# A conditioning stage on one core: caps moved from VectorE to ScalarE, forward scans made in place

## The chip, the cores and the metric

One Trainium2 chip, one of its cores. The metric is the device time of one execution in microseconds (us); lower is better. Engines: PE is TensorE, DVE VectorE, ACT ScalarE, POOL GpSimd, SP the queue that issues most transfers.

## What is computed

Four batches of 512 tokens with 512 channels pass through one layer: a bidirectional recurrence over the tokens ("conditioning"), a gated recurrence with four 512x512 projections, a second conditioning of the result, and a mixture of 8 experts with 2 chosen per token. Both conditionings share their input k = v = `fside`, and differ in the per-channel vectors w and u. The change lies in them:

```
tf    = sigmoid(sum(cond))                       # one number per batch
decay = exp(-exp(w)) * (0.5 + 0.5 * tf)          # per channel and batch
ek    = exp(minimum(k, 30.0));  ekv = ek * v
df, nf = forward scans  a = a * decay + ek (ekv)
db, nb = the same scans from the last token to the first
euk   = exp(minimum(u + k, 30.0))
num   = nf + nb - ekv + euk * v
den   = df + db - ek + euk
out   = sigmoid(r) * num / maximum(den, 1e-8) * (0.8 + 0.2 * tf)
```

All of it is float32.

## The kernel before, in words

The program has two phases. The first makes the two conditionings, the gated recurrence, the logits and the places of the tokens, and sends the rows to the experts' slots in HBM; the second computes the experts. The change is in the first alone.

**Units.** Channels lie on the 128 partitions, tokens along the free dimension, so a batch is four tiles of 128x512, called units here (u = 4b + ct, 16 in all). Since k doesn't depend on the layer, a unit makes both conditionings c = 0 and 1 together: four sums (numerator n = 0 and denominator n = 1 of each c) in `sums_even` or `sums_odd`, by the parity of the unit. Every other buffer of a unit is double too, except `recip0` and `scaled`.

**A unit, engine by engine.** PE transposes f into `ps_f`; ACT copies it to `kT` (`copy_f`, L539). DVE makes the caps (`caps`): min(k, 30) into `ek` (L745) and min(k + u, 30) into `euk` for each c (L747). ACT takes exp of both in place (`exps`, L552, L553). POOL multiplies by k: `ekv` (L332), `eukv` for each c (L334, L335). DVE scans backward over the tokens (`backward`, L784 for ek, L785 for ekv, for each c). The recurrence forward then runs over the backward sums: with b the backward sum, the two-sided sum s obeys s[t] = d * s[t-1] + (1 - d*d) * b[t], with s[0] = b[0]. So ACT writes (1 - d*d) * b to `scaled` (`scale`, L562, one instruction of 128x1022 for each c), and DVE scans it forward into `sums` (`fold`, L796, four scans of 511 columns). The per-channel decay is read from PSUM (`ps_decay`). DVE adds `euk` to both denominators (L800, L801) and takes the maximum with 1e-8 for both in one instruction (L803), which signals `s_den`. ACT makes a first reciprocal as exp(-ln(den)) (`first_reciprocal`, L572, L575); POOL adds the own term to the numerators and multiplies twice by it (`newton`, L343, L346, L347, for each c); DVE forms the quotient (`ratio`, L812) after a Newton step.

**Order.** Each engine runs a list written out by hand; semaphores join them. In a step DVE does, for the units s = 0 to 3: `backward`, `caps` of the next unit, `fold`, then the ratios of unit s - 1. ACT does `copy_f` of the next unit, `first_reciprocal` of unit s - 1, `scale` of s, `exps` of the next. POOL does `newton` of unit s - 1, then `products` of unit s + 1. Behind these lines stand the rest of the step: step b also makes the gates of batch b - 1 (PE `gate`, L428; ACT L590, L601; DVE `recurrence`, L829 to L832) and the output rows and routing of batch b - 2 (DVE `residual` after the first backward, L839; `second_out` after fold 1, L844; `select` after fold 2, L853 to L868; `place` at the end; POOL `dispatch`, L365). At a step's end stand the last ratios and `first_out` (L821). Steps 0 to 3 have conditioning, steps 1 to 4 gates, steps 2 to 5 the tail. Steps 2 and 3 are one loop in the program.

The list on ACT around the change (`unit(s)` in `step`, L647 to L654) is:

```
copy_f(b if s + 1 < CT else b + 1, (s + 1) % CT)
if s >= 1: first_reciprocal(b, s - 1)
scale(b, s)
exps(b if s + 1 < CT else b + 1, (s + 1) % CT)
```

## Time and profile before

| | |
|---|---|
| time, median of 3 runs | 1264.4 us (1262.67 to 1265.08) |
| the profiled execution's own time, its span | 1265.84 us, 1263.7 us |
| busy: PE, weight loads, DVE, ACT, POOL | 1051.8, 830.8, 693.6, 527.8, 306.5 us |
| mean granted clock of TensorE, share of full speed | 0.939 |
| 14 to 88 us (step 0): DVE busy | 68.7 of 74.0 us |
| 260 to 350 us (step 3): DVE busy | 82.8 of 90.0 us |
| 350 to 420 us (steps 4 and 5 in part): PE, DVE busy | 68.7, 34.8 of 70.0 us |
| first expert matmul | 475 us |

Times in the profile are from the span's start. A busy share over the whole span mixes the two phases: PE is busy for most of the second, DVE for most of the first four steps. An instruction's time in the trace includes what it waited for inside the engine, so the same form can have two lengths.

### The profile page before, as it was taken

The numbers are of one execution on the slowest core, as the hardware profiler recorded it, in microseconds if no ns is written. First come the engines' busy times: TensorE is split into PE (matmuls) and PEld (weight loads), VectorE is DVE, ScalarE is ACT, GpSimd is POOL, SyncE is SP. The second block draws the span as 40 slices with busy tenths as digits, with TensorE's granted clock in tenths as the row PEclk, the third lists the DMA queues.
The fourth block names the chain that finished last, engine by engine and source line by source line (L and its number), as shares of the span: only waits on it lengthen the run. The fifth ranks groups of instructions, "written<-read, shape, count | busy, mean of one in ns | idle before, by whom it ended". The sixth has DMA issues, their size and how long they took to land.

```text
span 1263.7 us, 16714 instructions
## 1 busy us (share of the span) xinstructions
PE 1051.8 (83%) x5058; PEld 830.8 (66%) x5059; DVE 693.6 (55%) x1026; ACT 527.8 (42%) x845; POOL 306.5 (24%) x251
## 2 busy tenths in 40 slices
PE   1045886886899719999999999999897997999994
PEld 0022343433457519998999899889786886988883
DVE  6989899899872523334333433445454343333553
ACT  5354645835844202334233333334454333333453
POOL 4767727547530230001000200020202002000202
PEclk9998897987998759999999999999998998999997
DMA  7151150111021351114311622253535135211721
GB/s 245 39 160 34 65 182 32 67 68 66 0 82 43 145 202 68 66 67 127 89 66 66 151 101 97 103 115 133 157 130 171 66 133 140 69 66 66 189 87 20
DMA packets 63420, 125.53 MB, mean 99 GB/s; under 512 B 4726, under 2 KB 4762, under 8 KB 63384
## 3 DMA queue, kind: packets, MB, share of 16 engines
q1 hardware_dynamic: 54728, 107.91, 24.5%
q0 software_dynamic: 8656, 17.13, 6.7%
q8 instruction: 24, 0.39, 0.1%
q14 instruction: 12, 0.10, 0.0%
HBM read 93.04 MB, written 35.22 MB: 101 GB/s over the span
## 4 chain that ended last, share of the span: by engine, by line
PE 57%; issue 4%; ACT 1%; POOL 0%; DVE 0%; DVEq 0%; ACTq 0%; POOLq 0%
PE ps_h L1099 9%; PE ps_h L1101 9%; PE ps_y L1110 9%; PE ps_h L1100 9%; PE ps_y L1111 9%; PE ps_y L1112 9%; PE ps_t L1073 1%; POOL out_dram L1052 0%; ACT xh L1209 0%; ACT y L1216 0%; ACT w1h L1181 0%; DVE w1l L1232 0%; DVEq L1154 0%; DVE hl L1271 0%; DVEq L105 0%
## 5 line engine op out<-in xcount | busy, mean ns | idle before, releaser
L1099 PE MATMUL ps_h<-xh,w1h 128*128 128x320 f32 (+3 forms) x768 | 250.7, 326 | 38.2 <-issue 36.3
L1101 PE MATMUL ps_h<-xh,w1l 128*128 128x320 f32 (+3 forms) x768 | 246.3, 321 | 0.0
L1100 PE MATMUL ps_h<-xl,w1h 128*128 128x320 f32 (+3 forms) x768 | 246.2, 321 | 0.0
L1271 DVE SCALAR_TENSOR_TENSOR hl<-ps_h,hh 128x320 fp32r<-128x320 f32 (+1 forms) x192 | 107.0, 558 | 229.0 <-ACT hh L1205 224.3
L1052 POOL DMA_INDIRECT out_dram<-y,token x40 | 63.2, 1579 | 692.2 <-ACT y L1216 514.9
L1110 PE MATMUL ps_y<-w2h,hh 128*128 128x512 f32 (+1 forms) x528 | 206.8, 392 | 1.0 <-DVE hl L1271 1.0
L1111 PE MATMUL ps_y<-w2h,hl 128*128 128x512 f32 (+1 forms) x528 | 206.8, 392 | 0.0
L1112 PE MATMUL ps_y<-w2l,hh 128*128 128x512 f32 (+1 forms) x528 | 206.0, 390 | 0.0
L1205 ACT ACTIVATE hh<-ps_h 128x320 fp32r<-128x320 f32 (+1 forms) x192 | 94.3, 491 | 266.8 <-PE ps_h L1101 266.6
L1235 DVE TENSOR_TENSOR w2l<-raw,w2h 128x512 fp32r<-128x512 f32 x128 | 88.5, 692 | 198.0 <-ACT w2h L1184 197.1
L428 PE MATMUL ps_mm<-r1T,wm 128*128 (+1 forms) x320 | 162.3, 659 | 21.3 <-ACT z_in L590 14.4
L1099 PEld LDWEIGHTS ps_h<-xh,w1h 128*128 128x128 f32 x768 | 148.0, 193 | 47.2 <-issue 38.2
L1184 ACT ACTIVATE w2h<-raw 128x512 fp32r x128 | 80.8, 631 | 211.6 <-PE ps_y L1112 211.6
L1100 PEld LDWEIGHTS ps_h<-xl,w1h 128*128 128x128 f32 x768 | 148.0, 193 | 5.0
L1101 PEld LDWEIGHTS ps_h<-xh,w1l 128*128 128x128 f32 x768 | 147.6, 192 | 2.7
L428 PEld LDWEIGHTS ps_mm<-r1T,wm 128*128 128x128 f32 x320 | 66.0, 215 | 96.9 <-issue 79.5
L1112 PEld LDWEIGHTS ps_y<-w2l,hh 128*128 128x128 f32 (+1 forms) x528 | 96.6, 183 | 24.3
L1111 PEld LDWEIGHTS ps_y<-w2h,hl 128*128 128x128 f32 (+1 forms) x528 | 96.6, 183 | 19.7
L1110 PEld LDWEIGHTS ps_y<-w2h,hh 128*128 128x128 f32 (+1 forms) x528 | 96.6, 183 | 19.3 <-DVE hl L1271 1.3
L1232 DVE TENSOR_TENSOR w1l<-raw,w1h 128x512 fp32r<-128x512 f32 x128 | 88.4, 690 | 16.2 <-ACT w1h L1181 12.4
L1181 ACT ACTIVATE w1h<-raw 128x512 fp32r x128 | 79.8, 623 | 0.0
L365 POOL DMA_INDIRECT slots<-r_rows,dest x32 | 35.0, 1095 | 103.9 <-DVE dest L890 61.2
(190 smaller groups left out, 1291.4 us busy)
## 6 DMA issues: line engine op xcount, KB each, us to landing
raw<-in_L_ffn_w_dram SPq DMA_DIRECT2D x64, 1024.0 KB
slots<-r_rows SPq DMA_DIRECT2D x8, 1302.5 KB, 15.2
rows<-slots SPq DMA_DIRECT2D x8, 1302.5 KB, 9.1
f_rows<-in_fside_BxSxS_dram SPq DMA_DIRECT2D x5, 1024.0 KB, 5.4
rows<-in_x_dram SPq DMA_DIRECT2D x4, 1024.0 KB, 6.2
out_dram<-x_rows SPq DMA_DIRECT2D x4, 1024.0 KB, 5.3
slots<-r_rows POOLq DMA_DIRECT2D x1, 1302.5 KB
rows<-slots SPq DMA_DIRECT2D x5, 260.5 KB, 3.9
```

Source lines behind the costliest of these rows:

```text
L428: last = nc.tensor.matmul(ps_mm[:, k % 3, :], wm[:, m, dt, e * P:(e + 1) * P], r1T[:, bass.ds(b % 2, 1), dt, :].rearrange("p o t -> p (o t)"),
L1099: nc.tensor.matmul(o, w1h[:, j, dt, :], xh[:, dt, lo:hi], start=(dt == 0), stop=False)
L1100: nc.tensor.matmul(o, w1h[:, j, dt, :], xl[:, dt, lo:hi], start=False, stop=False)
L1101: last = nc.tensor.matmul(o, w1l[:, j, dt, :], xh[:, dt, lo:hi], start=False, stop=(dt == CT - 1))
L1110: nc.tensor.matmul(ps_y[0:m, i, :], hh[:, j, tok], w2h[:, j], start=first, stop=False)
L1111: nc.tensor.matmul(ps_y[0:m, i, :], hl[:, j, tok], w2h[:, j], start=False, stop=False)
L1112: done = nc.tensor.matmul(ps_y[0:m, i, :], hh[:, j, tok], w2l[:, j], start=False, stop=last)
L1184: a.activation(w2h[:, (j + 1) % 2], raw2[:, bass.ds((c + (j + 1) // FC) % 2, 1), (j + 1) % FC] .rearrange("p o n -> p (o n)"), ACT.Copy).t ...
L1205: a.activation(hh[:, j % 2, lo:hi], ps_h[:, bank, 0:hi - lo], ACT.Relu).then_inc(s_hh, 1 if wide else 2)
L1232: v.tensor_tensor(w1l[:, j % 2], raw1[:, bass.ds((c + j // 2) % 2, 1), :, (j + 2) % FC * P:((j + 2) % FC + 1) * P] .rearrange("p o t q -> ...
L1235: v.tensor_tensor(w2l[:, (j + 1) % 2], raw2[:, bass.ds((c + (j + 1) // FC) % 2, 1), (j + 1) % FC] .rearrange("p o n -> p (o n)"), w2h[:, ( ...
L1271: v.scalar_tensor_tensor(out=hl[:, j % 2, lo:hi], in0=ps_h[:, bank, 0:hi - lo], scalar=0.0, in1=hh[:, j % 2, lo:hi].bitcast(F32), op0=ALU.max,
```

## The change

The sums are carried divided by 1 - d*d. The forward scan then reads the backward sum itself, s[t] = d * s[t-1] + b[t], in place; only column 0 of the four sums is multiplied by 1 / (1 - d*d) first (new L802). `scale` and its buffer go. The own term gets the same divisor inside its exp: `euk` is exp(30 - ln(1 - d*d) - relu(30 - u - k)), and the floor 1e-8 becomes a number per channel (`den_min`), so the maximum is one instruction for each c. 1 - d*d is bounded below by 1e-10. The caps are relu(30 - k) and relu(30 - u - k) on ACT straight from `ps_f`, three instructions ahead of the copy in `copy_f`; the exps have scale -1 and a bias, and three instructions instead of two. `copy_f` of unit u waits in addition until unit u - 2 has signalled `s_den`, since it fills buffers that `fold` reads. A few small instructions are added to the setup, and the first exps wait for them.

```diff
--- before.py
+++ after.py
@@ -32,6 +32,8 @@
 ROW = C + NE + 1
 NO_TOKEN = 1 << 20
 CAPV, DEN_MIN = 30.0, 1e-8
+
+MD2_MIN = 1e-10
 FT = DFF // P
 FC = 4
 NC = FT // FC
@@ -87,7 +89,7 @@
 
         with ExitStack() as early:
             cond_buffers = [early.enter_context(nc.sbuf_tensor(name, [P, 4, T], F32))
-                            for name in ("scaled", "k_and_exp_k", "euk", "eukv", "sums_even", "sums_odd")]
+                            for name in ("spare", "k_and_exp_k", "euk", "eukv", "sums_even", "sums_odd")]
         with ExitStack() as early:
             gate_parts = [early.enter_context(nc.sbuf_tensor(name, [P, CT, C], F32R)) for name in (
                 "r1_high", "r1_low", "w_decay_high", "w_decay_low", "w_gate_high", "w_gate_low")]
@@ -149,6 +151,13 @@
     decay = sb("decay", [P, B * 2 * CT])
     one_m = sb("one_m", [P, B * 2 * CT])
     one_md2 = sb("one_md2", [P, B * 2 * CT])
+
+    inv_md2 = sb("inv_md2", [P, B * 2 * CT])
+    inv_pair = sb("inv_pair", [P, B * CT, 2, 1])
+    own_bias = sb("own_bias", [P, (B + 1) * 2 * CT])
+    den_min = sb("den_min", [P, B * 2 * CT])
+    cap_u = sb("cap_u", [P, 2, CT])
+    cap_k = sb("cap_k", [P, 1])
     bdec = sb("bdec", [P, CT])
 
     x_rows = rows[:, 0:TT, 0:C]
@@ -160,7 +169,6 @@
     ekv = sb("ekv", [P, 2, T])
     euk, eukv = (cond_buffers[n][:].rearrange("p (r c) t -> p r c t", r=2) for n in (2, 3))
     sums = [cond_buffers[n][:].rearrange("p (c n) t -> p c n t", c=2) for n in (4, 5)]
-    scaled = cond_buffers[0][:].rearrange("p (c n) t -> p c n t", c=2)
     recip0 = sb("recip0", [P, 2, T])
     r1T = sb("r1T", [P, 2, CT, T])
     ratio2 = sb("ratio2", [P, 2, CT, T])
@@ -204,9 +212,9 @@
     s_pool_setup, s_template, s_consts = sem("pool_setup"), sem("template"), sem("consts_ready")
     s_setup_v, s_setup_a = sem("setup_dve"), sem("setup_act")
     s_f_tp, s_x_tp, s_k, s_xT = sem("f_transposed"), sem("x_transposed"), sem("k_ready"), sem("xT_ready")
-    s_caps, s_ek, s_euk, s_ekv, s_eukv = sem("caps_ready"), sem("ek_ready"), sem("euk_ready"), sem("ekv_ready"), sem("eukv_ready")
-    s_bwd, s_scaled, s_den, s_ln, s_rec, s_newton, s_ratio = (
-        sem("bwd_done"), sem("scaled_ready"), sem("den_ready"), sem("ln_ready"), sem("recip_ready"),
+    s_ek, s_euk, s_ekv, s_eukv = sem("ek_ready"), sem("euk_ready"), sem("ekv_ready"), sem("eukv_ready")
+    s_bwd, s_den, s_ln, s_rec, s_newton, s_ratio = (
+        sem("bwd_done"), sem("den_ready"), sem("ln_ready"), sem("recip_ready"),
         sem("newton_ready"), sem("ratio_ready"))
     s_own = sem("numerator_own_term")
     s_gh, s_gl = sem("gate_operands_high"), sem("gate_operands_low")
@@ -218,6 +226,7 @@
     s_route, s_shift, s_pexp, s_sel, s_pos, s_dest, s_count = (
         sem("route_steps"), sem("shift_ready"), sem("prob_exp"), sem("sel_ready"), sem("pos_done"), sem("dest_ready"), sem("count_done"))
 
+    SETUP_MD2 = 17
     N_V = 9
     N_VEC = N_V + 1
     ROUTE_STEPS = 17 + 2 * TT
@@ -534,9 +543,14 @@
         def copy_f(b, ct):
             u = b * CT + ct
             act.wait_ge(s_f_tp, u + 1)
+            r = ct % 2
             if at_least(u, 2):
                 act.wait_ge(s_eukv, u - 1)
-            a.activation(kT[:, ct % 2], ps_f[:], ACT.Copy).then_inc(s_k, 1)
+                act.wait_ge(s_den, u - 1)
+            a.activation(ek[:, r], ps_f[:], ACT.Relu, scale=-1.0, bias=cap_k[:])
+            for c in range(2):
+                a.activation(euk[:, r, c], ps_f[:], ACT.Relu, scale=-1.0, bias=cap_u[:, c, ct:ct + 1])
+            a.activation(kT[:, r], ps_f[:], ACT.Copy).then_inc(s_k, 1)
 
         def copy_x(b, ct):
             act.wait_ge(s_x_tp, b * CT + ct + 1)
@@ -547,20 +561,14 @@
                          ACT.Copy).then_inc(s_xT, 1)
 
         def exps(b, ct):
+
             u, r = b * CT + ct, ct % 2
-            act.wait_ge(s_caps, u + 1)
-            a.activation(ek[:, r], ek[:, r], ACT.Exp).then_inc(s_ek, 1)
-            a.activation(euk[:, r], euk[:, r], ACT.Exp).then_inc(s_euk, 1)
-
-        def scale(b, ct):
-
-            u, r = b * CT + ct, ct % 2
-            if at_least(u, 1):
-                act.wait_ge(s_den, u)
+            act.wait_ge(s_k, u + 1)
+            a.activation(ek[:, r], ek[:, r], ACT.Exp, scale=-1.0, bias=cap_k[:]).then_inc(s_ek, 1)
             for c in range(2):
-                act.wait_ge(s_bwd, 2 * u + c + 1)
-                a.activation(scaled[:, c, :, 1:T], sums[r][:, c, :, 1:T], ACT.Copy,
-                             scale=one_md2[:, col(b, c, ct)]).then_inc(s_scaled, 1)
+                last = a.activation(euk[:, r, c], euk[:, r, c], ACT.Exp, scale=-1.0,
+                                    bias=own_bias[:, col(b, c, ct)])
+            last.then_inc(s_euk, 1)
 
         def first_reciprocal(b, ct):
 
@@ -649,7 +657,6 @@
                     copy_f(b if s + 1 < CT else b + 1, (s + 1) % CT)
                     if s >= 1:
                         first_reciprocal(b, s - 1)
-                    scale(b, s)
                     exps(b if s + 1 < CT else b + 1, (s + 1) % CT)
 
             if cond:
@@ -714,12 +721,14 @@
         setup = Steps(act, s_setup_a, 0)
         setup.do(a.activation(ew[:], vec[:, W1C:W2C + 1, :], ACT.Exp))
         setup.do(a.activation(ew[:], ew[:], ACT.Exp, scale=-1.0))
-        act.wait_ge(s_setup_v, 2)
+        act.wait_ge(s_setup_v, 5)
         setup.do(a.activation(tf[:], tf[:], ACT.Sigmoid))
         act.preload_act_table_set("natural_log_exp_and_others")
         copy_f(0, 0)
+        act.wait_ge(s_setup_v, SETUP_MD2)
+        setup.do(a.activation(own_bias[:, 0:B * 2 * CT], one_md2[:], ACT.Ln))
+        act.wait_ge(s_consts, 2)
         exps(0, 0)
-        act.wait_ge(s_consts, 2)
         step(0, True, False, False)
         step(1, True, True, False)
         with act.Fori(2, B) as b:
@@ -736,20 +745,12 @@
         v = nc.vector
         d0 = lambda b, c, ct, n: ps_decay[:, col(b, c, ct)].to_broadcast([P, n])
 
-        def caps(b, ct):
-
-            u, r = b * CT + ct, ct % 2
-            dve.wait_ge(s_k, u + 1)
-            if at_least(u, 2):
-                dve.wait_ge(s_den, u - 1)
-            v.tensor_scalar(ek[:, r], kT[:, r], CAPV, None, ALU.min)
-            for c in range(2):
-                last = v.tensor_scalar(euk[:, r, c], kT[:, r], vec[:, U1C + c, ct:ct + 1], CAPV, ALU.add, ALU.min)
-            last.then_inc(s_caps, 1)
-
         setup = Steps(dve, s_setup_v, 0)
         dve.wait_ge(s_vt, 1)
         setup.do(v.tensor_copy(vec[:].rearrange("p n t -> p (n t)"), ps_small[:, 0:N_V * CT]))
+        setup.mark(v.memset(cap_k[:], CAPV))
+        setup.mark(v.memset(own_bias[:, B * 2 * CT:], 0.0))
+        setup.mark(v.tensor_scalar(cap_u[:], vec[:, U1C:U2C + 1], -1.0, CAPV, ALU.mult, ALU.add))
         dve.wait_ge(s_vec, 16 * N_VEC)
         setup.mark(v.tensor_reduce(tf[:], vec_cond.rearrange("p (b d) -> p b d", b=B), AX.X, ALU.add))
         setup.mark(v.tensor_tensor(bdec[:], vec[:, BDEC], vec[:, DBIAS], ALU.add))
@@ -761,14 +762,21 @@
         for b in range(B):
             setup.mark(v.tensor_scalar(decay[:, b * 2 * CT:(b + 1) * 2 * CT], ew[:].rearrange("p c t -> p (c t)"),
                                        half_tf[:, b:b + 1], None, ALU.mult))
-        caps(0, 0)
         setup.wait()
         setup.mark(v.tensor_copy(ps_decay, decay[:]))
         setup.mark(v.tensor_scalar(one_m[:], decay[:], -1.0, 1.0, ALU.mult, ALU.add))
         setup.wait()
 
-        v.scalar_tensor_tensor(out=one_md2[:], in0=decay[:], scalar=1.0, in1=one_m[:], op0=ALU.add,
-                               op1=ALU.mult).then_inc(s_consts, 1)
+        setup.do(v.scalar_tensor_tensor(out=one_md2[:], in0=decay[:], scalar=1.0, in1=one_m[:], op0=ALU.add, op1=ALU.mult))
+        setup.do(v.tensor_scalar(one_md2[:], one_md2[:], MD2_MIN, None, ALU.max))
+        assert setup.n == SETUP_MD2, setup.n
+        setup.do(v.reciprocal(inv_md2[:], one_md2[:]))
+        setup.mark(v.tensor_scalar(den_min[:], inv_md2[:], DEN_MIN, None, ALU.mult))
+        for c in range(2):
+            setup.mark(v.tensor_copy(inv_pair[:, :, c].rearrange("p (b t) o -> p b (t o)", b=B),
+                                     inv_md2[:].rearrange("p (b c t) -> p b c t", b=B, c=2)[:, :, c]))
+        dve.wait_ge(s_setup_a, 4)
+        v.tensor_scalar(own_bias[:], own_bias[:], -1.0, CAPV, ALU.mult, ALU.add).then_inc(s_consts, 1)
 
         v.memset(r2_rows[:, 0], 0.0).then_inc(s_template, 1)
         dve.wait_ge(s_template, 1)
@@ -788,19 +796,25 @@
 
 
             u, r = b * CT + ct, ct % 2
-            steps = Steps(dve, s_fold, 4 * u)
+            steps = Steps(dve, s_fold, 5 * u)
+            dve.wait_ge(s_bwd, 2 * u + 2)
+            first = sums[r][:, :, :, 0]
+            steps.do(v.tensor_tensor(first, first, inv_pair[:, bass.ds(b * CT + ct, 1)].rearrange("p b c o -> p (b c) o")
+                                     .to_broadcast([P, 2, 2]), ALU.mult))
             for c in range(2):
-                dve.wait_ge(s_scaled, 2 * u + c + 1)
-                for n in range(2):
+                for n in (1, 0):
                     s = sums[r][:, c, n]
-                    ins = v.tensor_tensor_scan(s[:, 1:T], d0(b, c, ct, T - 1), scaled[:, c, n, 1:T], s[:, 0:1], ALU.mult, ALU.add)
+                    ins = v.tensor_tensor_scan(s[:, 1:T], d0(b, c, ct, T - 1), s[:, 1:T], s[:, 0:1], ALU.mult, ALU.add)
                     if n == 1:
                         steps.mark(ins)
             steps.wait()
-            steps.mark(v.tensor_tensor(sums[r][:, 0, 1], sums[r][:, 0, 1], euk[:, r, 0], ALU.add))
-            steps.mark(v.tensor_tensor(sums[r][:, 1, 1], sums[r][:, 1, 1], euk[:, r, 1], ALU.add))
+            dve.wait_ge(s_euk, u + 1)
+            for c in range(2):
+                steps.mark(v.tensor_tensor(sums[r][:, c, 1], sums[r][:, c, 1], euk[:, r, c], ALU.add))
             steps.wait()
-            v.tensor_scalar(sums[r][:, :, 1], sums[r][:, :, 1], DEN_MIN, None, ALU.max).then_inc(s_den, 1)
+            for c in range(2):
+                last = v.tensor_scalar(sums[r][:, c, 1], sums[r][:, c, 1], den_min[:, col(b, c, ct)], None, ALU.max)
+            last.then_inc(s_den, 1)
 
         def ratio(b, ct, c):
 
@@ -909,7 +923,6 @@
                     if gates and not cond:
                         gate_operands()
                 if cond:
-                    caps(b if s + 1 < CT else b + 1, (s + 1) % CT)
                     fold(b, s)
                 if tail and s == 1:
                     second_out(b - 2)
```

The order of DVE's instructions in the second unit of step 0 (odd buffers), before:

```order
L784 SCALAR_TENSOR_TENSOR sums_odd<-ps_decay,k_and_exp_k 128x512
L785 SCALAR_TENSOR_TENSOR sums_odd<-ps_decay,ekv 128x512
L784 SCALAR_TENSOR_TENSOR sums_odd<-ps_decay,k_and_exp_k 128x512
L785 SCALAR_TENSOR_TENSOR sums_odd<-ps_decay,ekv 128x512
L745 TENSOR_SCALAR k_and_exp_k<-k_and_exp_k 128x512
L747 TENSOR_SCALAR euk<-k_and_exp_k,vec 128x512 x2
L796 SCALAR_TENSOR_TENSOR sums_odd<-ps_decay,sums_odd,scaled 128x511 x4
L800 TENSOR_TENSOR sums_odd<-sums_odd,euk 128x512
L801 TENSOR_TENSOR sums_odd<-sums_odd,euk 128x512
L803 TENSOR_SCALAR sums_odd<-sums_odd 128x2x512
```

The same place now (the list writes a scan as SCALAR_TENSOR_TENSOR):

```order
L792 SCALAR_TENSOR_TENSOR sums_odd<-ps_decay,k_and_exp_k 128x512
L793 SCALAR_TENSOR_TENSOR sums_odd<-ps_decay,ekv 128x512
L792 SCALAR_TENSOR_TENSOR sums_odd<-ps_decay,k_and_exp_k 128x512
L793 SCALAR_TENSOR_TENSOR sums_odd<-ps_decay,ekv 128x512
L802 TENSOR_TENSOR sums_odd<-sums_odd,inv_pair 128x4
L807 SCALAR_TENSOR_TENSOR sums_odd<-ps_decay,sums_odd 128x511 x4
L813 TENSOR_TENSOR sums_odd<-sums_odd,euk 128x512 x2
L816 TENSOR_SCALAR sums_odd<-sums_odd,den_min 128x512 x2
```

The three caps between backward and forward scans are gone, a product of four elements stands there, and the maximum is split.

ACT's instructions for the same unit, before:

```order
L539 ACTIVATE k_and_exp_k<-ps_f 128x512
L572 ACTIVATE recip<-sums_even 128x512 x2
L575 ACTIVATE recip<-recip 128x512 x2
L562 ACTIVATE scaled<-sums_odd,one_md 128x2x511 x2
L552 ACTIVATE k_and_exp_k<-k_and_exp_k 128x512
L553 ACTIVATE euk<-euk 128x1024
```

And now:

```order
L550 ACTIVATE k_and_exp_k<-ps_f,cap_k 128x512
L552 ACTIVATE euk<-ps_f,cap_u 128x512 x2
L553 ACTIVATE k_and_exp_k<-ps_f 128x512
L580 ACTIVATE recip<-sums_even 128x512 x2
L583 ACTIVATE recip<-recip 128x512 x2
L567 ACTIVATE k_and_exp_k<-k_and_exp_k,cap_k 128x512
L569 ACTIVATE euk<-euk,own_bias 128x512 x2
```

Three instructions stand ahead of the reciprocal of the unit before, the scaling is gone, and one exp has become two.

## Rows read from the trace of the kernel before

**Rows 1.** Steps 1, 2: us, busy PE, PEld, DVE, ACT, POOL, clock, DMA, GB/s.

```profile
88.00:168.00 80.00, 59.38 (x141) 26.43 (x140) 74.26 (x75) 45.91 (x63) 47.45 (x36) 0.89 0.28 91
168.00:260.00 92.00, 73.89 (x244) 38.81 (x243) 85.63 (x103) 54.67 (x75) 48.84 (x36) 0.91 0.18 61
```

**Rows 2.** Groups by line, 0 to 420 us (count, busy us, mean ns, idle before).

```profile
L747 DVE TENSOR_SCALAR euk<-k_and_exp_k,vec 128x512 f32<-128x512 f32 x34 | 32.0, 980 | 0.0
...
L745 DVE TENSOR_SCALAR k_and_exp_k<-k_and_exp_k 128x512 f32<-128x512 f32 x17 | 13.6, 802 | 2.4 <-ACT k_and_exp_k L539 2.4
```

**Rows 3.** DVE in order of time (start, length, instruction): L803 in steps 1 and 2.

```profile
98.34 0.69 DVE L803 TENSOR_SCALAR sums_even<-sums_even 128x1024 f32<-128x1024 f32 x1
...
113.69 0.69 DVE L803 TENSOR_SCALAR sums_odd<-sums_odd 128x1024 f32<-128x1024 f32 x1
...
129.81 0.69 DVE L803 TENSOR_SCALAR sums_even<-sums_even 128x1024 f32<-128x1024 f32 x1
...
147.21 0.69 DVE L803 TENSOR_SCALAR sums_odd<-sums_odd 128x1024 f32<-128x1024 f32 x1
...
184.49 0.69 DVE L803 TENSOR_SCALAR sums_even<-sums_even 128x1024 f32<-128x1024 f32 x1
...
199.87 0.69 DVE L803 TENSOR_SCALAR sums_odd<-sums_odd 128x1024 f32<-128x1024 f32 x1
...
218.31 0.69 DVE L803 TENSOR_SCALAR sums_even<-sums_even 128x1024 f32<-128x1024 f32 x1
...
237.43 0.69 DVE L803 TENSOR_SCALAR sums_odd<-sums_odd 128x1024 f32<-128x1024 f32 x1
```

**Rows 4.** DVE in order of time: caps of two units, a ratio, step 1.

```profile
91.39 0.87 DVE L747 TENSOR_SCALAR euk<-k_and_exp_k,vec 128x512 f32<-128x512 f32 x2
...
103.42 1.39 DVE L745 TENSOR_SCALAR k_and_exp_k<-k_and_exp_k 128x512 f32<-128x512 f32 x1
104.74 2.88 DVE L747 TENSOR_SCALAR euk<-k_and_exp_k,vec 128x512 f32<-128x512 f32 x2
...
114.90 1.76 DVE L812 SCALAR_TENSOR_TENSOR ratio<-sums_even 128x512 f32<-128x512 f32 x1
```

**Rows 5.** POOL in order of time, a unit of step 1.

```profile
100.81 1.27 POOL L346 TENSOR_TENSOR sums_even<-sums_even,recip 128x512 f32<-128x512 f32 x1 [0.42 <-ACT recip L575]
...
109.60 1.26 POOL L334 TENSOR_TENSOR eukv<-euk,k_and_exp_k 128x512 f32<-128x512 f32 x1
110.82 1.26 POOL L335 TENSOR_TENSOR eukv<-euk,k_and_exp_k 128x512 f32<-128x512 f32 x1
```

**Rows 6.** ACT in order of time, a unit of step 1.

```profile
93.78 0.67 ACT L590 ACTIVATE z_in<-ps_mm,vec 128x512 f32<-128x512 f32 x1
94.35 0.58 ACT L539 ACTIVATE k_and_exp_k<-ps_f 128x512 f32<-128x512 f32 x1
99.06 1.15 ACT L572 ACTIVATE recip<-sums_even 128x512 f32<-128x512 f32 x2 [4.13 <-DVE sums_even L803]
```

**Rows 7.** DVE in order of time, step 2.

```profile
200.48 2.35 DVE L844 SCALAR_TENSOR_TENSOR sig<-ratio,neg_scale,sig 128x2048 f32<-128x2048 f32 x1
...
206.41 1.22 DVE L784 TENSOR_TENSOR_SCAN sums_even<-ps_decay,k_and_exp_k 128x512 f32<-128x512 f32 x1 [0.23 <-DVE ratio L812]
...
219.61 0.78 DVE L858 TENSOR_TENSOR prob<-logit,top 128x32 f32<-128x32 f32 x1
```

**Rows 8.** DVE in order of time: the first unit's adds, step 3.

```profile
276.56 1.86 DVE L800 TENSOR_TENSOR sums_even<-sums_even,euk 128x512 f32<-128x512 f32 x1
278.35 0.68 DVE L801 TENSOR_TENSOR sums_even<-sums_even,euk 128x512 f32<-128x512 f32 x1
```

**Rows 9.** End of step 1: ACT, then DVE, in order of time.

```profile
163.21 0.60 ACT L539 ACTIVATE k_and_exp_k<-ps_f 128x512 f32<-128x512 f32 x1
...
167.26 2.34 DVE L821 SCALAR_TENSOR_TENSOR r1T<-r1T,neg_scale,sig 128x2048 f32<-128x2048 f32 x1
```

**Rows 10.** POOL in order of time, its first product.

```profile
13.77 1.27 POOL L332 TENSOR_TENSOR ekv<-k_and_exp_k 128x512 f32<-128x512 f32 x1 [11.28 <-ACT k_and_exp_k L552]
```

## The prediction

> **What bounds the kernel now.** I began with the chain that ended last: it names only lines of the expert phase and nothing of the phase that the change touches, so I went to the busy times by stage. In steps 1 and 2, VectorE (DVE) is busy 74.3 of 80.0 us and 85.6 of 92.0, TensorE (PE), ACT and POOL clearly less [rows 1]. So every microsecond that DVE's row of instructions gets shorter there moves all that follows. The expert phase begins when the rows are dispatched; the change doesn't touch it, and I take its length as it is.
>
> Then I read DVE's instructions in order of time, one unit (a batch's 128 channels) after another. I write den(u) for the end of `fold(u)`, the L803 of unit u. From den to den the units of step 1 take 15.35, 16.12 and 17.40 us, those of step 2 take 15.38, 18.44 and 19.12 [rows 3]. Within the unit that ends at 114.38, the backward scans take 4.4 us (99.03 to L745 at 103.42), the caps 4.1, and from there to L803 at 113.69 it is 6.15 [rows 3, 4]: two own adds of 0.65 (L801) [rows 8], so 4.8 for the forward scans. A step's first unit has the short caps (1.1, as in the first of rows 4) and so takes 4.5 + 1.1 + 4.8 + 2.0 = 12.4 us.
>
> Last I asked why the same instruction has two durations. The three caps (L745, L747) of a unit take 1.39 + 2.88 us in one unit, while the second pair of another costs 0.87 [rows 4]; their means are 802 and 980 ns [rows 2]. The long ones lie where POOL runs its multiplications one after another, 1.23 us from start to start, from 1.8 us after den until 13.0 us after it [rows 5]. The ratio L812 takes 1.76 us where POOL has just begun [rows 4], L858, with 32 elements, 0.78 us [rows 7]. So a DVE instruction of these kinds waits until POOL's instruction ends, and POOL's next one waits for it. Scans whose first operand is in PSUM don't wait: L784 to L796 keep one duration.
>
> That is the reading on which the forecast rests: DVE and POOL take turns, and what DVE saves beside a busy POOL it may have to wait for a few instructions later.
>
> **Edit 1: caps and exps on ACT.** DVE loses 3 instructions per unit, 2.76 us by the means [rows 2], 44 us over 16 units. ACT gets three Relus from PSUM. The nearest row is L590, from PSUM with a bias of its own: 0.67 us, 0.57 to the next start [rows 6]; so 1.7 us more in `copy_f`, and a split exp costs 0.2. ACT loses two scalings of 1.15 each, so its total stays. What changes is when it works: `copy_f(u+1)` now waits for den(u-1), since the own add L800 still reads the buffer that the Relus fill, and `first_reciprocal(u-1)` is queued behind it on ACT. Before, it began 0.03 us after den and POOL's L346 1.78 us after den [rows 5, 6]. Now 3 x 0.57 + 0.48 = 2.2 us pass first: L346 begins at den + 4.0.
>
> The Trainium skill ("ScalarE: Activation LUTs", rules for kernel authors) speaks against this edit: relu belongs on VectorE, which is faster per element. By that rule alone the edit would lose time. Alone, two caps on DVE take 0.87, one ACT instruction of that kind 0.67 [rows 4, 6]: three on one engine's own path would cost 1.7 for 1.1, 16 x 0.6 = 10 us, 1274 in all. But in this profile DVE is the bound [rows 1], so I count what leaves DVE.
>
> **Edit 2: scans in place.** Removed: the two scalings; they lay beside the caps, so nothing of them is on DVE. Added: L802, four elements per partition, which must wait until the last backward scan has ended (0.1) and costs 0.2: 0.3 us, and up to 1.23 more if POOL is in the middle of an instruction. The scans keep 4.8 us. The maximum with a floor per channel is two instructions for one, 0.72 for 0.61. The order of the two scans in a pair saves under 0.1. A unit of DVE alone is then 4.4 (backward) + 0.35 + 4.8 + 1.3 + 0.7 = 11.6 us.
>
> **Putting them together**, with t = 0 at den(u-1):
> - POOL has own add, then from 4.0 eight instructions of 1.23 and a gap of 0.14: two multiplies, own add, two multiplies, three products of unit u+1. It ends at 14.0 if DVE never stops it.
> - *Second unit of a step.* DVE: backward until 4.5, L802 waits until 5.3, scans until 10.2. Now it asks for four instructions (two own adds, two maxima) while POOL runs until 14. In turns, each POOL instruction pushed by an own add by some 0.45: den at 15.4. Before it was 15.35. **Gain -0.1**: 4.1 us of caps leave and all come back as waits. Before, POOL's L335 ended at 112.1 and DVE's two adds, the 1.3 us ahead of L803 at 113.69, found POOL idle [rows 3, 5].
> - *Third unit.* Two ratios first (2.4 us, the second waits for POOL as now). Scans end at 12.6, POOL at 14.0; one or two adds wait; den at 15.9 against 16.12. **Gain 0.2** in steps 0 and 1. In steps 2 and 3 L844 and two ratios stand ahead: the next backward starts 5.85 us after den [rows 7]. With L346 only at 4.0 the second ratio gets in before it, 4.7 instead of 5.85; scans end at 14.5, as POOL stops; den at 16.5 against 18.44. **Gain 1.9**.
> - *Fourth unit.* Step 0 (without gates) like its third, 0.2. In step 1 den to den is 17.40 because ACT waited for PE's gate tile and POOL ran late, into the caps; ACT, no longer held by the scaling and the caps, feeds PE earlier, so 15.9: **gain 1.5**. In steps 2 and 3 routing comes first (next backward 4.4 after den); scans end at 14.0, POOL too; den at 16.1 against 19.12: **gain 3.0**.
> - *First unit of a step*: POOL idle, caps 1.1 less L802 and the split: **gain 0.8** in steps 0 to 2; in step 3 an own add already waited a whole POOL instruction (1.86 against 0.68 for L801) beside the products after the dispatch [rows 8], and two will: **0.15**.
> - *Ends of steps.* ACT's first Exp of the next step now needs no DVE, so POOL multiplies while DVE still runs L832, L821 and the last ratio. At the end of step 1 ACT's first copy begins at 163.21 and DVE ends L821 at 169.6 [rows 9]: with 2.3 for the copies and 0.6 for the Exp POOL's three products fall into 166 to 170, three DVE instructions wait one each: **-3.0**. At the end of step 0 one: **-1.05**. In steps 2 and 3 POOL waits for the dispatch: 0.
> - *Start.* POOL's first product waits for ACT until 13.77 [rows 10]. New chain: four ACT copies from 11.2 (to 13.5), Ln, a small DVE instruction, Exp: 14.6. **-0.85**.
>
> Step 3 was read less closely: apart from its first unit I take it as step 2. Sum: step 0 1.1, step 1 2.4, step 2 5.6, step 3 4.95, ends -4.05, start -0.85: 9.2 us. The profiled execution took 1265.8 (span 1263.7), so 1256.6 for one like it; the median of the runs is 1264.4, 1.4 lower, and from it I forecast **1255**. Bounds: no waits at all given back, 16 x (2.76 - 0.45) = 37 less 0.85, so 1228; one POOL instruction more (1.23) in each of the 12 units that are not first, 14.8, so 1270. I take the worked schedule, since its turns are those that rows 4, 7 and 8 show.
>
> A second rule of the skill ("SBUF — State Buffer", who interferes with whom) makes the pair of ports an exclusive lock whose loser waits for the whole instruction, and says that issue order decides. Rows 8 agree (L800 asked just before POOL's next and lost). It says nothing of fair turns; if POOL always won, the slow rival below is its time.
>
> **Rivals.**
> - *The waits don't come back* (37 us at most; half of it likelier). For: POOL's 14 us leave slack in units of 16. Against: all its work lies exactly where DVE's adds are now. 1228 to 1247.
> - *Slower.* DVE loses the pair once more per unit, at L802 or the first add, as L800 did. From 0.75 us per unit on (9.2 / 12) the gain is gone; the full price gives 1270. For: L802 adds one request per unit in the middle of POOL's run. Against: in rows 4 the caps did get every second turn.
> - *ACT and PE hold steps 2 and 3*: ACT, now waiting for den, copies gate sums later, and the 10 us of these steps stay. Against: PE is busy 73.9 of 92 [rows 1]. 1264.
>
> **Numbers.** My case (1248 to 1261) 0.55; half of the waits 0.13 (1242 to 1248); all saved 0.08; no change 0.11; slower 0.13. About 0.2% (2.5 us) is what a measurement of this kernel can tell from none. Leaving out the fastest case and most of the slowest gives 1241 to 1265.
>
> **What would show it.** POOL's first multiply by the reciprocal at den + 4.0; the second unit still near 15.4 us; own adds of 1.2 to 1.9 us instead of 0.7; fourth units of steps 2 and 3 near 16; the expert phase as long as before. If adds stay at 0.7 and units fall to 12 or 13 us, the reading of turns is wrong; if L802 alone takes over 1.2 us everywhere, the slow rival holds.

## The result and the profile after

The changed kernel takes 1258.5 us (median of 20 runs, 1248.4 to 1261.0), the kernel before 1263.3 (20 runs, 1256.1 to 1266.1): ratio 0.995, 95% interval 0.993 to 0.997. It is faster by 4.8 us; the forecast was 1255, range 1241 to 1265. The profiled execution took 1258.88 us, its span is 1256.8, against 1265.84 and 1263.7 before. Four of its 20 runs took 1248.4 to 1250.1 and two of before 1256.1; no run here shows what set them apart.

The head of the page of the changed kernel:

```profile
span 1256.8 us, 16771 instructions
...
PE 1047.8 (83%) x5058; PEld 829.5 (66%) x5059; DVE 683.8 (54%) x1016; ACT 526.4 (42%) x882; POOL 311.5 (25%) x251
```

DVE lost 9.8 us of busy time where 44 us of caps left it, ACT's total stayed, POOL's grew by 5. Its busy times in steps 1 and 2, in windows moved to where these steps now lie (columns as in [rows 1]), are hardly lower than before, with three caps a unit gone: 74.1 of 80 us (74.3) and 83.8 of 92 (85.6).

```profile
90.00:170.00 80.00, 57.86 (x139) 25.75 (x138) 74.11 (x71) 45.13 (x71) 49.34 (x37) 0.87 0.34 110
173.00:265.00 92.00, 78.29 (x249) 41.05 (x247) 83.83 (x114) 53.65 (x83) 48.34 (x36) 0.89 0.12 41
```

Where the time went shows in order of time. DVE, the second unit of step 1 and its neighbours (L802 is the new scaling of four elements, L813 the own adds, L816 the maxima, L826 the ratios). It answers to [rows 3, 4]:

```profile
97.60 1.27 DVE L813 TENSOR_TENSOR sums_even<-sums_even,euk 128x512 f32<-128x512 f32 x2
98.90 0.88 DVE L816 TENSOR_SCALAR sums_even<-sums_even,den_min 128x512 f32<-128x512 f32 x2
...
103.06 1.20 DVE L793 TENSOR_TENSOR_SCAN sums_odd<-ps_decay,ekv 128x512 f32<-128x512 f32 x1
104.30 0.86 DVE L802 TENSOR_TENSOR sums_odd<-sums_odd,inv_pair 128x4 f32<-128x4 f32 x1
105.19 4.80 DVE L807 TENSOR_TENSOR_SCAN sums_odd<-ps_decay,sums_odd 128x511 f32<-128x511 f32 x4
109.91 2.54 DVE L813 TENSOR_TENSOR sums_odd<-sums_odd,euk 128x512 f32<-128x512 f32 x2
112.48 2.77 DVE L816 TENSOR_SCALAR sums_odd<-sums_odd,den_min 128x512 f32<-128x512 f32 x2
```

The scans end at 109.99, 10.2 us after den, yet den comes only at 115.25: two adds take 2.54 where they take 1.27 beside an idle POOL (first line), two maxima 2.77 where they take 0.88. POOL over the same stretch (compare [rows 5]):

```profile
103.86 1.27 POOL L355 TENSOR_TENSOR sums_even<-sums_even,recip 128x512 f32<-128x512 f32 x1 [2.73 <-ACT recip L583]
...
108.97 1.26 POOL L356 TENSOR_TENSOR sums_even<-sums_even,recip 128x512 f32<-128x512 f32 x1
110.19 1.71 POOL L341 TENSOR_TENSOR ekv<-k_and_exp_k 128x512 f32<-128x512 f32 x1
111.86 1.71 POOL L343 TENSOR_TENSOR eukv<-euk,k_and_exp_k 128x512 f32<-128x512 f32 x1
113.53 1.45 POOL L344 TENSOR_TENSOR eukv<-euk,k_and_exp_k 128x512 f32<-128x512 f32 x1
```

It starts at den + 4.08 and works until den + 15.2; where DVE's adds and maxima ask, its own instructions stretch from 1.26 to 1.71 us (1.67 from start to start instead of 1.23). Both engines are late by each other. The end of step 1, DVE, where three instructions wait (0.69, 2.35 and 0.68 without):

```profile
166.03 1.59 DVE L846 TENSOR_TENSOR z_gate<-z_gate,z_in 128x512 f32<-128x512 f32 x1
167.54 3.35 DVE L835 SCALAR_TENSOR_TENSOR r1T<-r1T,neg_scale,sig 128x2048 f32<-128x2048 f32 x1
170.82 1.75 DVE L826 SCALAR_TENSOR_TENSOR ratio<-sums_odd 128x512 f32<-128x512 f32 x1
```

All intervals, read in this way from the order of time (us; first scan to first den; den to den three times; last den to the next step's first scan, in step 3 to the end of the last ratio):

| step | before | after | forecast gain | measured |
|---|---|---|---|---|
| start (first scan) | 15.17 | 15.73 | -0.85 | -0.56 |
| 0 | 12.43; 15.36, 16.10, 16.10; 11.44 | 12.44; 15.43, 15.99, 16.00; 12.50 | 1.1, end -1.05 | 0.1, end -1.06 |
| 1 | 12.43; 15.35, 16.12, 17.40; 22.22 | 11.69; 15.47, 16.02, 16.01; 25.21 | 2.4, end -3.0 | 2.1, end -2.99 |
| 2 | 15.06; 15.38, 18.44, 19.12; 25.35 | 14.27; 15.46, 16.66, 16.48; 25.43 | 5.6 | 5.1 |
| 3 | 16.28; 15.38, 18.45, 19.60; 22.30 | 16.54; 15.45, 16.66, 16.39; 22.39 | 4.95 | 4.6 |
| last ratio of step 3 | 355.48 | 348.22 | 9.2 | 7.26 |

Behind step 3 the change touches nothing, but the rest didn't keep its length. In step 4 a stretch of PE work ran at a granted clock of 0.72 before (of 2.4 GHz; a part of it at 1.2) and at 1.00 after; in both kernels PE had been busy without a gap ahead of it. Windows of before, then of after:

```profile
372.00:380.00 8.00, 8.00 (x33) 5.35 (x31) 1.31 (x1) 3.26 (x6) 0.00 (x0) 1.00 0.27 99
380.00:392.00 12.00, 12.00 (x60) 10.70 (x60) 2.19 (x19) 1.74 (x3) 0.00 (x0) 0.72 0.06 24
```

```profile
366.00:373.00 7.00, 7.00 (x29) 4.83 (x28) 0.36 (x1) 2.32 (x4) 0.00 (x0) 1.00 0.28 108
373.00:383.00 10.00, 10.00 (x67) 8.92 (x66) 2.19 (x19) 2.46 (x4) 0.00 (x0) 1.00 0.08 30
```

So DVE's first recurrence instruction of the last gate stage, at 405.54 before, came 10.2 us earlier, and the first expert matmul 9.05 us earlier (in the chain of waits: "465.12 9.63 issue" before it, so 474.75, against 465.70). From there to the end of the span the profiled execution of before took 788.95 us and that of after 791.1. The span came out 6.9 us shorter.

The 3 us of step 4 don't follow the change. From step 3's last ratio to that recurrence instruction the profiled executions took 46.9 to 47.8 us where the granted clock stayed at 1.00 (after, e1, e3, e5, e8 below), and 47.4, 48.5, 48.5, 50.1 and 51.2 us where it fell for a while (e2, e4, e6, before, e7). e1 is the kernel before with one edit, e7 the changed kernel with one wait more; in before, after and e7 PE was busy through all of it.

### The profile page after: what moved, and what is told of

Read it like the earlier page. It is cut to its first block, busy times and chain, and to the rows that moved or that the text cites. A ratio compares the mean times of both kernels' runs of the same rounds, so it can differ in the third digit from the quotient of the medians.

```text
span 1256.8 us, 16771 instructions
## 1 busy us (share of the span) xinstructions
PE 1047.8 (83%) x5058; PEld 829.5 (66%) x5059; DVE 683.8 (54%) x1016; ACT 526.4 (42%) x882; POOL 311.5 (25%) x251
## 4 chain that ended last, share of the span: by engine, by line
PE 57%; issue 4%; ACT 1%; POOL 0%; DVE 0%; DVEq 0%; ACTq 0%; POOLq 0%
PE ps_h L1112 10%; PE ps_h L1113 9%; PE ps_h L1114 9%; PE ps_y L1123 9%; PE ps_y L1124 9%; PE ps_y L1125 9%; PE ps_t L1086 1%; POOL out_dram L1065 0%; ACT xh L1222 0%; ACT y L1229 0%; ACT w1h L1194 0%; DVE w1l L1245 0%; DVEq L1167 0%; DVE hl L1284 0%; ACTq L1167 0%
## 5 line engine op out<-in xcount | busy, mean ns | idle before, releaser
L437 PE MATMUL ps_mm<-r1T,wm 128*128 (+1 forms) x320 | 151.3, 621 | 9.8 <-ACT z_in L598 6.0
L437 PEld LDWEIGHTS ps_mm<-r1T,wm 128*128 128x128 f32 x320 | 61.7, 201 | 78.2 <-issue 70.0
L451 PE MATMUL ps_mm<-z_gate,wm 128*128 128x512 f32 x96 | 49.9, 652 | 26.0 <-DVE z_gate L846 26.0
```

Source lines behind the costliest of these rows:

```text
L437: last = nc.tensor.matmul(ps_mm[:, k % 3, :], wm[:, m, dt, e * P:(e + 1) * P], r1T[:, bass.ds(b % 2, 1), dt, :].rearrange("p o t -> p (o t)"),
```

## The experiments

Times of before on the same chips: 1264.9 us for the first four, 1264.4 for the last four. "Last ratio" is that of step 3: 355.48 before, 348.22 after.

**Each edit alone.** `e1_caps_alone` is the kernel before with the Relus in `copy_f` and the exps that go with them; the scaled copies stay. `e2_inplace_alone` is the other half. Of e1's edit, the main lines:

```diff
-                caps(b if s + 1 < CT else b + 1, (s + 1) % CT)
+            a.activation(ek[:, r], ps_f[:], ACT.Relu, scale=-1.0, bias=cap_k[:])
+            for c in range(2):
+                a.activation(euk[:, r, c], ps_f[:], ACT.Relu, scale=-1.0, bias=cap_u[:, c, ct:ct + 1])
```

> Edit 1 alone on the kernel before: caps as relu and exps on ACT (own term exp(30 - relu(30 - u - k))), scalings and out-of-place scans kept. Theory (turns on the shared ports): the 4.1 us of caps that leave the second unit of a step come back as waits of the two own adds and of the maximum while POOL works, so den(0) to den(1) in step 1 stays at 15 to 16 us (before 15.35, changed kernel 15.47), each own add 1.2 to 1.9 us; the last ratio of step 3 ends at 346 to 352 us (before 355.5, changed kernel 348.2), time 1255 to 1261. Rival (the loss is in what the changed kernel adds, the product on column 0 and the split maximum): without them the second unit falls to about 12 us, the own adds stay at 0.7 us, the last ratio ends before 335, time near 1240.

Measured: 1264.2 us, ratio 0.999 (0.998 to 1.000); last ratio at 354.64. The second unit took 15.6: the four microseconds of caps came back as waits, as expected, and the rival's 12 us is out. The total was missed (1255 to 1261 us and a last ratio at 346 to 352 were expected). Steps 2 and 3 read 15.6, 16.9 and 21.0 (21.2): their third units gained 1.5, their fourth lost 1.9 and 1.6. DVE in the fourth unit of step 2 (L795 scans, L800 and L801 own adds, L803 maximum), then ACT and POOL:

```profile
226.96 4.80 DVE L795 TENSOR_TENSOR_SCAN sums_odd<-ps_decay,sums_odd,scaled 128x511 f32<-128x511 f32 x4 [2.05 <-ACT scaled L571]
231.79 1.81 DVE L800 TENSOR_TENSOR sums_odd<-sums_odd,euk 128x512 f32<-128x512 f32 x1
233.53 1.75 DVE L801 TENSOR_TENSOR sums_odd<-sums_odd,euk 128x512 f32<-128x512 f32 x1
235.31 1.64 DVE L803 TENSOR_SCALAR sums_odd<-sums_odd 128x1024 f32<-128x1024 f32 x1
```

```profile
219.91 0.69 ACT L599 ACTIVATE z_dec<-ps_mm,bdec 128x512 f32<-128x512 f32 x1 [5.52 <-PE ps_mm L430]
...
225.46 1.27 POOL L348 TENSOR_TENSOR sums_even<-sums_even,recip 128x512 f32<-128x512 f32 x1 [8.16 <-ACT recip L584]
```

ACT stood idle until PE's gate tile came, 4.0 us after den at 215.95. Its Relus, the reciprocal and the scaling, queued in this order, came late: the scans wait for the scaling, POOL's multiplications start 9.5 us after den, and the adds fall into POOL's run. In the changed kernel ACT begins the same Relus 0.3 us after den and the unit takes 16.5. So the caps pay where the scaling has gone too; whether it was the scaling that made PE's gate tile late wasn't tried.

> Edit 2 alone: scans in place, product on column 0, floor per channel, divisor in the exp; the caps stay on DVE and ACT's copy and reciprocal keep their old places. Theory: nothing leaves DVE, the product on column 0 waits for a POOL instruction (0.9 us) in the middle of the unit and the maximum costs 0.2 more, so about 1 us per unit in 12 units and 0.5 in 4: the last ratio of step 3 ends at 363 to 370 us, time 1270 to 1278. Rival (scans in place are worth something by themselves, since ACT's scaling no longer stands between the scans): last ratio at 350 to 355, time at or under 1263.

Measured: 1271.3 us, ratio 1.0045 (1.003 to 1.006); last ratio at 361.61. Slower, as expected: the time lies in its range, the last ratio a little ahead of it. The second unit of step 1 grew by 0.2 only, less than expected; the third by 0.2, the fourth by 0.5, and in step 2 the fourth took 20.5. The reason given for the loss failed: the product of four elements took 0.15 or 0.16 us in 15 of the 16 units. In the second unit of step 1 it fell, at 108.77, into 1.0 us in which POOL stood idle, waiting for ACT's exp of the caps. So neither half pays: 0.8 us gained by one, 6.1 lost by the other up to the last ratio, and together 7.3 gained. The whole isn't the sum of its parts; the fourth units of steps 2 and 3 show it most, 21.0 and 21.2 us with the first edit alone, 20.5 and 19.7 with the second, 16.5 and 16.4 with both.

**ACT's order.** The reciprocal of the unit before goes ahead of `copy_f`, in the changed kernel:

```diff
-                    copy_f(b if s + 1 < CT else b + 1, (s + 1) % CT)
                     if s >= 1:
                         first_reciprocal(b, s - 1)
+                    copy_f(b if s + 1 < CT else b + 1, (s + 1) % CT)
```

> The changed kernel with one swap in ACT's list: first_reciprocal(s-1) ahead of copy_f of the next unit. Theory: POOL's first multiply by the reciprocal begins at den + 1.8 instead of 4.0, so POOL is done 2.2 us earlier and DVE's own adds wait less: second unit of a step 13.4 to 14.2 us instead of 15.47; third and fourth units of steps 0 and 1 about 14.8 instead of 16.0. In steps 2 and 3 the third and fourth units get 1 to 1.5 us longer, since POOL now works beside the ratios and the product on column 0. Together 6 to 8 us: last ratio of step 3 at 340 to 343, time 1250 to 1253. Rival (DVE's adds wait for something else than POOL's last products): units unchanged, time 1258.

Measured: 1256.7 us, ratio 0.993 (0.992 to 0.995); last ratio at 346.63. Steps 0 and 1 did what was expected or a little better: 13.7, 14.2, 14.2 (14.8 was expected for the third and fourth). In steps 2 and 3 the second unit fell to 13.9, but the fourth rose from 16.4 to 21.3, where 1 to 1.5 us were expected, and the third from 16.7 to 17.7. So both totals missed their ranges (340 to 343, 1250 to 1253). In the fourth unit POOL's multiplications now began 1.9 us after den instead of 4.3, beside the routing's small DVE instructions. DVE, fourth unit of step 2:

```profile
209.95 1.17 DVE L876 CAST top_f<-top_i 128x32 f32<-128x32 uint32 x1
211.16 2.43 DVE L878 TENSOR_TENSOR oh<-expert_no,top_f 128x32 f32<-128x32 f32 x2
...
214.06 1.43 DVE L826 SCALAR_TENSOR_TENSOR r1T<-sums_odd 128x512 f32 x1
215.41 1.75 DVE L826 SCALAR_TENSOR_TENSOR ratio<-sums_odd 128x512 f32 x1
```

The same instructions in the changed kernel, beside an idle POOL:

```profile
220.87 0.18 DVE L876 CAST top_f<-top_i 128x32 f32<-128x32 uint32 x1
221.08 0.29 DVE L878 TENSOR_TENSOR oh<-expert_no,top_f 128x32 f32<-128x32 f32 x2
...
221.85 0.69 DVE L826 SCALAR_TENSOR_TENSOR r1T<-sums_odd 128x512 f32 x1
222.46 0.68 DVE L826 SCALAR_TENSOR_TENSOR ratio<-sums_odd 128x512 f32 x1
```

Two comparisons of 32 elements take 2.43 us: each waits for a whole instruction of POOL. These rows hold the whole loss: the cast is 1.0 us longer, the comparisons 2.1, the two ratios 0.7 and 1.1, 4.9 us in all, and the backward scans begin 9.4 us after den instead of 4.5. Nothing of it comes back, because in the changed kernel DVE's adds already met no wait there (1.28 us for two). In these rows the price of a meeting doesn't depend on DVE's size, so the worst place for POOL's run is beside many small DVE instructions.

**POOL held at a step's start**, on top of this order (e4) and, later, on the changed kernel alone (e7):

```diff
+                if s == 0 and at_least(b, 1):
+                    pool.wait_ge(s_ratio, 2 * CT * b)
                 if s < CT:
                     products(b * CT + (s + 1), (s + 1) % CT)
```

> As e3, and POOL waits for the last ratio of the step before ahead of the first products of a step (steps 1 to 3). Theory: at the ends of steps 0 and 1 DVE's last instructions find POOL idle again, 1.0 and 3.0 us back (end of step 1, den(3) to the first scan of step 2, 22.2 us instead of 25.2); nothing in steps 2 and 3, where the dispatch stands ahead. Last ratio of step 3 at 336 to 339, time 1246 to 1249. Rival (the 3 us at the end of step 1 are ACT's longer row of copies, not POOL): end of step 1 unchanged at 25.2, time as e3.

Measured: 1252.0 us, ratio 0.989 (0.988 to 0.991); last ratio at 342.77; ends of steps 0 and 1 at 11.43 and 22.22. The ends are as expected, and the rival that puts the 3 us down to ACT's copies is out. The wait gave 3.9 us on top of e3; the totals expected (336 to 339, 1246 to 1249) were missed by what e3 had missed.

> The changed kernel with one wait more: in steps 1 to 3 POOL starts the new step's first products only after DVE's last ratio of the step before. If the two terms for the ends of steps (1.05 and 3.0 us) are what POOL's early products cost DVE, the ends of steps 0 and 1 go from 12.5 and 25.2 us back to 11.4 and 22.2, units stay as they are, the last ratio ends 3.5 to 4.1 us earlier, near 344.3, and the time is near 1254. Rival: the products come late then and the first unit of the next step grows by as much: no gain, 348 and 1258.

Measured: 1254.5 us, ratio 0.992 (0.991 to 0.994); last ratio at 344.30; ends 11.43 and 22.22, and no unit changed by over 0.15. The end of step 1, DVE and then POOL, with the three instructions at their own lengths again:

```profile
165.10 0.69 DVE L848 TENSOR_TENSOR z_gate<-z_gate,z_in 128x512 f32<-128x512 f32 x1
165.71 2.34 DVE L837 SCALAR_TENSOR_TENSOR r1T<-r1T,neg_scale,sig 128x2048 f32<-128x2048 f32 x1
167.97 0.68 DVE L828 SCALAR_TENSOR_TENSOR ratio<-sums_odd 128x512 f32<-128x512 f32 x1
```

```profile
168.89 1.27 POOL L341 TENSOR_TENSOR ekv<-k_and_exp_k 128x512 f32<-128x512 f32 x1 [13.78 <-DVE ratio L828]
```

A semaphore wait that holds POOL back saves 3.9 us, and costs nothing: DVE's backward scans of the new step don't need those products, and its first units took 11.69 and 14.28 us as without the wait.

**One product of POOL left out**, all of DVE's work kept. The second cap's product isn't computed, its own add reads the first's:

```diff
-            g.tensor_tensor(eukv[:, r, 0], euk[:, r, 0], kT[:, r], ALU.mult)
-            g.tensor_tensor(eukv[:, r, 1], euk[:, r, 1], kT[:, r], ALU.mult).then_inc(s_eukv, 1)
+            g.tensor_tensor(eukv[:, r, 0], euk[:, r, 0], kT[:, r], ALU.mult).then_inc(s_eukv, 1)
```

> The changed kernel with one of POOL's three products per unit left out (the one of the second cap; its own add reads the first cap's product instead, so that part of the computation is left out). DVE's instructions are all kept. Turns theory: POOL's row sets the second unit everywhere and the third and fourth of steps 0 and 1, so each is shorter by about one POOL instruction: 15.45 to about 14.2 us, 16.0 to about 14.8; the third and fourth of steps 2 and 3 (16.7, 16.4) hardly move, by 0 to 0.5. End of step 1 about 1 us shorter. Sum about 11 us: the last ratio ends near 337 us, the time is near 1248. Rival, by which DVE's adds and maxima are long by themselves or through what they read: units as in the changed kernel, last ratio at 348, time 1258.

Measured: units 14.42 to 14.47 where they were 15.43 to 15.47, and 14.93 to 14.96 where 16.0; the third and fourth of steps 2 and 3 stayed at 16.66 and 16.38; the end of step 1 is 1.07 shorter, and so is the first unit of step 3 by 1.2, which was not expected; last ratio at 337.75. The time, 1174.7 us, says nothing of this: other sums route other tokens, and the expert phase has 704 matmuls of its first line where it had 768. The units are the result, and they fit. In the second unit of step 1 nothing of DVE's work was taken, and it ends 1.0 us earlier:

```profile
102.25 4.80 DVE L806 TENSOR_TENSOR_SCAN sums_odd<-ps_decay,sums_odd 128x511 f32<-128x511 f32 x4
106.97 2.54 DVE L812 TENSOR_TENSOR sums_odd<-sums_odd,euk 128x512 f32<-128x512 f32 x2
109.55 1.77 DVE L815 TENSOR_SCALAR sums_odd<-sums_odd,den_min 128x512 f32<-128x512 f32 x2
```

**The new instruction left out.** Without L802 the first elements stay unscaled:

```diff
-            steps.do(v.tensor_tensor(first, first, inv_pair[:, bass.ds(b * CT + ct, 1)].rearrange("p b c o -> p (b c) o")
-                                     .to_broadcast([P, 2, 2]), ALU.mult))
```

> The changed kernel without L802, the multiplication of four first elements (that part of the computation is left out). DVE has an instruction of 0.2 us less per unit that in places takes 0.9 us. Turns theory: where POOL's row sets the end of the unit (second units, third and fourth of steps 0 and 1) nothing comes back: 15.4 and 16.0 us stay within 0.15. First units lose 0.3 to 0.9 us, the third and fourth of steps 2 and 3 about 0.3 to 0.5. Sum 3 to 4 us: last ratio near 345, time near 1255. Rival, by which each microsecond taken from DVE counts: 16 times 0.3 to 0.9, that is 5 to 14 us, last ratio at 334 to 343, second units at 15.1 or less.

Measured: 1257.7 us, ratio 0.995 (0.994 to 0.997); last ratio at 346.74, 1.5 earlier, about half of what was expected. Second, third and fourth units moved by 0.13 at most, in steps 2 and 3 too, where 0.3 to 0.5 was expected; the first units of steps 0, 1 and 2 lost 0.94, 0.2 and 0.2. The second unit of step 1 shows where it went:

```profile
103.27 4.80 DVE L804 TENSOR_TENSOR_SCAN sums_odd<-ps_decay,sums_odd 128x511 f32<-128x511 f32 x4
107.99 3.43 DVE L810 TENSOR_TENSOR sums_odd<-sums_odd,euk 128x512 f32<-128x512 f32 x2
111.45 2.78 DVE L813 TENSOR_SCALAR sums_odd<-sums_odd,den_min 128x512 f32<-128x512 f32 x2
```

The scans start 0.9 us sooner after their backward scans, and the two adds take 3.43 for 2.54: all 0.89 is returned.

**Best of both orders.** The reciprocal ahead of the copies, POOL held at a step's start, but behind the copies as in the changed kernel for the third and fourth units of steps 2 and 3 (the lines of ACT's order; POOL's wait is as above):

```diff
+                    ahead = s == 1 or not tail
+                    if s >= 1 and ahead:
+                        first_reciprocal(b, s - 1)
                     copy_f(b if s + 1 < CT else b + 1, (s + 1) % CT)
-                    if s >= 1:
+                    if s >= 1 and not ahead:
                         first_reciprocal(b, s - 1)
```

> The version with the reciprocal ahead of the copies and POOL's wait at a step's start, but in steps 2 and 3 the reciprocal stands ahead of the copies for the second unit alone; for the third and fourth it is behind them, as in the changed kernel. If the turns explain the long fourth units (21.3 us where POOL's multiplications fall beside the routing's small instructions), these go back to those of the changed kernel: steps 2 and 3 read about 13.9, 16.7, 16.5 us, steps 0 and 1 stay at 13.7, 14.2, 14.2, the ends at 11.4 and 22.2. The last ratio of step 3 then ends near 331 us (342.8 before this edit), the time is near 1240. Rival: the long fourth unit comes of ACT or PE being late after the shorter second unit: 19 to 21 us stay, the last ratio stays above 338 us and the time above 1248.

Measured: 1240.2 us, ratio 0.9815 (0.980 to 0.983); last ratio at 331.0; steps 0 and 1 at 13.7, 14.2 and 14.2, steps 2 and 3 at 13.9, 16.7 (16.8) and 16.4, ends 11.45 and 22.21. It beats both kernels: by 24 us the one before, by some 17 the changed one (by the two ratios). The routing's instructions, fourth unit of step 2, have their own lengths again:

```profile
205.13 0.18 DVE L881 CAST top_f<-top_i 128x32 f32<-128x32 uint32 x1
205.35 0.29 DVE L883 TENSOR_TENSOR oh<-expert_no,top_f 128x32 f32<-128x32 f32 x2
```

## Why the prediction was right, and where its terms were off

**DVE and POOL take turns**: shown from both sides. Work taken from DVE inside POOL's run is returned (e1: 15.6 us with the caps gone; e8: 0.86 us gone, 0.89 back). Work taken from POOL ends the unit earlier with DVE's instructions all kept (e6: 1.0 us for one product, about an instruction of 1.23). Moving the start of POOL's run moves the end of the unit (e3: start at den + 1.8 instead of 4.1, second unit 1.75 shorter). This also parts the 4.1 us of caps: with POOL starting where it did before the change, the second unit takes 13.7 us and not 15.35, so about 1.6 us of them are kept. That none is kept in the changed kernel comes of its own Relus ahead of the reciprocal, which start POOL 2.3 us later.

The first rival, waits that don't come back, is out. So is ACT or PE holding steps 2 and 3 of the changed kernel, whose fourth units fell to 16.4 or 16.5; in e1 just that happened. The slower rival is out too: L802 took at most 0.91 us, and no unit but the first of step 3 grew by more than 0.12.

**POOL starts at den + 4.0**: 4.08. **Second units**: forecast -0.1, measured -0.07 to -0.12. **Third and fourth**: 15.9 forecast in steps 0 and 1, 16.0 measured; in steps 2 and 3, 16.5 and 16.1 forecast, 16.66 and 16.4 to 16.5 measured. A part of it is the **maximum split in two**: 0.72 for 0.61 was forecast, and the pair of L816 takes 0.88 for L803's 0.69 [rows 3], also beside an idle POOL. That is 0.19 a unit instead of 0.11. In the fourth unit of step 2 the scans also ended 14.3 us after den, not 14.0. In step 3 the same gain of 3.0 was forecast and 3.2 measured, by luck: that unit had taken 19.60 before and not step 2's 19.12, and step 3 had been read less closely. For the **fourth unit of step 1** the forecast gave 1.5, because ACT would be held neither by the scaling nor by the caps; 1.4 came. Each edit alone left it at 17.35 (e1) and 17.9 (e2), where it had been 17.40 and both give 16.0, which fits that reason.

**Ends of steps**: forecast -1.05, -3.0, 0; measured -1.06, -2.99, -0.08, and e7 gave 4.1 back by removing their cause. The one part of the change that loses time was priced rightly, from one ACT row and one DVE row [rows 9]. **Start**: -0.85 forecast, -0.56 measured, as the copies ended at 13.1 instead of 13.5.

**First units** are the term that failed: 0.8 in steps 0 to 2 and 0.15 in step 3 were forecast; measured -0.01, 0.74, 0.79 and -0.26. The step of the argument was "POOL idle". In step 0 it wasn't. DVE and POOL there:

```profile
20.33 0.91 DVE L802 TENSOR_TENSOR sums_even<-sums_even,inv_pair 128x4 f32<-128x4 f32 x1
21.27 4.80 DVE L807 TENSOR_TENSOR_SCAN sums_even<-ps_decay,sums_even 128x511 f32<-128x511 f32 x4
```

```profile
19.95 1.26 POOL L341 TENSOR_TENSOR ekv<-k_and_exp_k 128x512 f32<-128x512 f32 x1 [0.94 <-ACT k_and_exp_k L567]
```

L802 asks at 20.33 while POOL multiplies until 21.2, and pays 0.7 for it; e8 shows that the instruction is worth 0.94 there. With ACT's exps ahead of DVE, POOL's products of the next unit come earlier everywhere, which the forecast used for the ends of steps and forgot here. In step 3 the pair of own adds takes 3.49, as forecast; it was priced too low by 0.4 with L802 and the maxima.

By the Trainium skill ("SBUF — State Buffer", who interferes with whom) the loser waits for the whole of the other's instruction and what issues first wins. The rows bear that out for a single meeting, down to four elements (L802). Over a run it comes out as turns: POOL's three products at 110.19 to 113.53 are 1.67 apart instead of 1.23, while DVE's adds and maxima each wait. By the Trainium skill ("ScalarE: Activation LUTs", rules for kernel authors) relu belongs on VectorE; its figure is for bf16, and this kernel is float32. The prediction's rows had given 1274 for three caps on an engine's own path. e1 measures that edit alone at no change (0.999): neither that loss nor the 44 us that left DVE.

**The sum**: 9.2 forecast to the end of step 3, 7.26 measured: first units 1.3 too high, the third and fourth units 0.8, ends and the rest 0.1, the start 0.3 the other way. From there the forecast counted the rest as of fixed length. In sum it was, 908.2 us before and 908.6 after, but by luck: step 4 gave back 3 us where the clock stayed at 1.00, of which 1 was gone by the first expert matmul, and the expert phase took 2.15 more. Over the nine profiled executions in which that phase does the same work (all but e6) it took 788.9 to 792.3 us, so two microseconds are the execution's own; what makes them wasn't found. The medians differ by 4.8 and not 6.9 since the profiled execution of before took 2.5 us more than the median of its 20 runs, and that of after only 0.4 more. The forecast of 1255 was 3.5 us low: 1.9 in the sum, 0.4 behind step 3, 1.2 in how the medians stand to the profiled executions. By the medians the gain is about half of the 9.2. And the range, 1241 to 1265, held the time before as well: the time alone says little for the reading of turns, the intervals and the experiments say it. What sets the rise and fall of the clock in step 4 wasn't tried.

## What to carry to other kernels

Where two engines take turns, as DVE and POOL here, count the work of both from the event that starts them. What is taken from one inside the other's run can be returned a few instructions later; what counts is when the run starts, how long it is, and what lies beside it: scans with a PSUM operand cost nothing there, many small instructions cost most. So look at the third engine that releases the run: here the order of two calls on ACT and one wait on POOL gave 17 us, while 44 us of work taken from the busiest engine gave 5. And try each edit alone before you judge: neither half of this change paid.
